# Four of eight feed-forward batches moved in slices into the second half of an attention loop

## What is computed

```python
def _L0_xattn_ref(hidden_states, key_value_states, ...):
    h_q = (rmsnorm(hidden_states) @ w_q.T).reshape(b, lq, H, DH)   # H = 32, DH = 128
    h_k = (key_value_states @ w_k.T).reshape(b, lk, H, DH)
    h_v = (key_value_states @ w_v.T).reshape(b, lk, H, DH)
    score = softmax(where(mask, h_q h_k^T + position_bias, -inf))
    return hidden_states + (score h_v) @ w_out.T

def _L0_ffn_ref(x, w_gate, w_up, w_down):          # HIDDEN 512, INTER 1376
    def fake_quant(t, axis):
        s = maximum(max(abs(t), axis) / 127, 1e-8)
        return clip(round(t / s), -128, 127) * s
    gate, up = qlinear(x, w_gate), qlinear(x, w_up)   # both operands fake_quant
    return qlinear(silu(gate) * up, w_down)

# third layer: per position, the 76 largest of 128 context channels (top_k) choose
# which rows of x are "crucial"; each part is reduced by max and mean over channels
```

## Time and profile before

| | |
|---|---|
| median of 3 runs | 1130.78 us (1128.15 to 1132.11) |
| the profiled execution | 1128.72 us |
| its span, first to last instruction | 1127.0 us |
| PE busy | 1005.8 us (89% of the span) |
| DVE busy | 697.8 us (62%) |
| ACT busy | 512.3 us (45%) |
| POOL busy | 496.3 us (44%) |
| mean granted clock of TensorE | 0.964 |

### The profile page before, as it was taken

How to read it: one execution, slowest core, us unless ns; L and a number is a source line. 1 busy time by engine, 2 the same in 40 slices (tenths; PEclk the granted TensorE clock), 3 DMA queues, 4 the chain that set the end, 5 groups by cost and what they waited for, 6 DMA issues and landing times. The chain is left out here.

```text
span 1127.0 us, 19424 instructions
## 1 busy us (share of the span) xinstructions
PE 1005.8 (89%) x6010; PEld 852.9 (76%) x6010; DVE 697.8 (62%) x1835; ACT 512.3 (45%) x1333; POOL 496.3 (44%) x370
## 2 busy tenths in 40 slices
PE   3798999999999999999999999999999976665455
PEld 2687888888888888888888888888888863332343
DVE  6676777777677677675444444444444479998375
ACT  2334344444434434444444444444444455767342
POOL 4544545454444455434444444444454412554200
PEclk8898999999999999999999999999999999999578
DMA  5222222222222223223222232223223100000001
GB/s 212 75 80 80 80 80 79 79 86 93 88 79 79 79 79 105 80 93 118 94 94 93 94 101 102 102 99 102 92 92 114 58 16 20 1 0 1 0 1 75
DMA packets 50325, 87.22 MB, mean 77 GB/s; under 512 B 6320, under 2 KB 15152, under 8 KB 50288
## 3 DMA queue, kind: packets, MB, share of 16 engines
q1 hardware_dynamic: 50288, 86.76, 23.3%
HBM read 84.64 MB, written 2.10 MB: 77 GB/s over the span
## 5 line engine op out<-in xcount | busy, mean ns | idle before, releaser
L632 ACT ACTIVATE prob<-score,neg_max 128x128 f32<-128x128 f32 x256 | 99.8, 391 | 140.6 <-DVE neg_max L899 140.5
L966 DVE TENSOR_TENSOR aT_lo<-pT,aT_hi 128x512 fp32r<-128x512 f32 x64 | 44.2, 691 | 179.2 <-ACT aT_hi L572 179.1
L1221 PE MATMUL pX<-wv_lo,cT_hi 128*128 128x256 f32 x512 | 151.4, 296 | 0.7 <-ACT v_sb L572 0.7
L464 POOL TENSOR_TENSOR wq_lo<-raw_q,wq_hi 128x512 fp32r<-128x512 f32 x64 | 92.2, 1441 | 130.7 <-ACT wq_hi L572 130.6
L1222 PE MATMUL pX<-wv_hi,cT_lo 128*128 128x256 f32 x512 | 145.9, 285 | 0.0
L1223 PE MATMUL pX<-wv_hi,cT_hi 128*128 128x256 f32 x512 | 145.9, 285 | 0.0
L472 POOL TENSOR_TENSOR b_mask<-b_raw,mask_add 128x512 f32<-128x512 f32 x64 | 74.7, 1168 | 151.2 <-DVE score L896 151.2
L464 POOL TENSOR_TENSOR wv_lo<-raw_v,wv_hi 128x1024 fp32r<-128x1024 f32 x32 | 76.9, 2402 | 109.0 <-ACT wv_hi L572 109.0
L572 ACT ACTIVATE v_sb<-pX 128x512 f32<-128x512 f32 x64 | 38.2, 597 | 175.7 <-PE pX L1223 175.7
L860 DVE COPY k_sb<-pX 128x512 f32<-128x512 f32 x64 | 44.1, 688 | 112.9 <-PE pX L1223 112.9
L1221 PE MATMUL pX<-xT_lo,wq_hi 128*128 128x512 f32 x256 | 107.3, 419 | 4.3 <-DVE xT_lo L848 4.3
(11 more groups left out here) (213 smaller groups left out, 2407.2 us busy)
## 6 DMA issues: line engine op xcount, KB each, us to landing
raw_q<-in_wq SPq DMA_DIRECT2D x64, 256.0 KB, 3.5
raw_k<-in_wk SPq DMA_DIRECT2D x64, 256.0 KB, 3.4
raw_v<-in_wv SPq DMA_DIRECT2D x32, 512.0 KB, 3.9
raw_o<-in_wo SPq DMA_DIRECT2D x64, 256.0 KB, 2.7
b_raw<-in_bias SPq DMA_DIRECT2D x64, 64.0 KB, 3.1
f_raw<-in_w_down SPq DMA_DIRECT2D x4, 688.0 KB, 6.5
g_raw<-in_w_gate SPq DMA_DIRECT2D x16, 172.0 KB
g_raw<-in_w_up SPq DMA_DIRECT2D x16, 172.0 KB
```

The costliest lines, as they stand in the source:

```text
L464: g.tensor_tensor(w_lo[c][:], w_raw[c][:], w_hi[c][:].bitcast(F32), ALU.subtract).then_inc(s_w_lo[c], 1)
L632: e = a.activation(prob[:, b, :], score[:, b, :], ACT.Exp, bias=neg_max[:, b:b + 1], accum_out=row_sum[:, b:b + 1])
L966: v.tensor_tensor(aT_lo[:], pT[:], aT_hi[:].bitcast(F32), ALU.subtract).then_inc(s_a_lo, 1)
L1221: mm(dst, lh, rl, start=start, stop=False, skip_group_check=lint)
```

## The change

In the words of its author: feed-forward of the first four batches put in slices between the projections of the second half of attention; gate and up rows quantised in the first half.

- **Rows.** The 32 blocks of w_gate and w_up go from steps 32 to 63 to steps 0 to 31 (rows_of_gate, ahead of the top-k round).
- **Top-k.** Four steps instead of two for two tiles, over both halves: one filling of pick (j = 0, where j = n mod 4), two rounds in steps j = 0 to 2, one in j = 3, each step's first one ahead of prob. It is filled from the split context (cT_hi, cT_lo) instead of cT_raw.
- **w_down.** Steps 32 to 35, with one buffer f_raw; block 0 is loaded in the first half, block i + 1 after the loads of step 33 + i and ScalarE's f_q of block i. Its transposes are in steps 33 to 36 (banks pT and pX1), the row of steps sd_row in step 37.
- **Feed-forward of batch t = 0 to 3** over steps 38 + 6t + r (turn(n, r)): r = -2 statistics, -1 y and its integers, 0 transposes of y into pT, 0 to 2 gate into pX1 behind the values, 1 to 3 up into pT behind the outputs, 3 silu, 4 product, maximum and integers, 5 transposes of h, 6 down projection into pX0 and xr, 7 and 8 normalisation to z, 9 its transposes, 10 split on GpSimd, 11 maxima and sums. The z part is done for batches 0 to 2; batch 3's z is left to the tail. Each piece that borrows a bank adds a wait for its reader (first_bank_free, key_bank_free).
- **Tail.** ffn_step for batches 4 to 7 only; residual now comes ahead of it; GpSimd computes z of batches 0 to 2 again into the array that lies over attention's. Steps 32 to 63 are written out, no longer a loop.

```diff
-        DOWN_STEPS = (H, H + 1, STEPS - 2, STEPS - 1)
+        FFN_FROM = H + 6
+        PERIOD = 6
+        DOWN_FROM = H
+        EARLY_Z = HB - 1
+        def turn(n, r):
+            t, rest = divmod(n - FFN_FROM - r, PERIOD)
+            return t if rest == 0 and 0 <= t < HB else None
...
@@ sync
+            for n in range(H, STEPS):
+                loads(n, n // 2, n % 2, n - H)
+                i = down_turn(n - 1)
+                if i is not None and i + 1 < KT:
+                    sp.wait_ge(s_f_q, i + 1)
+                    sp.dma_start(f_raw[:], w_down[(i + 1) * P:(i + 2) * P, :]).then_inc(s_f_in, 16)
...
@@ scalar
+                t = turn(n, 3)
+                if t is not None:
+                    act.wait_ge(s_e_gate, CHUNKS * (t + 1))
+                    a.activation(e_gate[:], e_gate[:], ACT.Silu).then_inc(s_e_silu, 1)
...
@@ vector
+            def early_bubble(n):
+                t = turn(n, -1)
+                if t is not None:
+                    dve.wait_ge(s_e_rstd, t + 1)
+                    v.tensor_scalar(y[:], xr[:, t, :], e_ymv[:, 0:1], e_yrs[:, 0:1], ALU.subtract, ALU.mult)
...
+                    v.tensor_scalar(y_mag[:], y[:], y_s[:, 2:3], MAGIC, ALU.mult, ALU.add).then_inc(s_e_y_mag, 1)
...
+                t = turn(n, 4)
+                if t is not None:
+                    dve.wait_ge(s_e_silu, t + 1)
+                    v.tensor_tensor(e_up[:], e_gate[:], e_up[:], ALU.mult)
+                    dve.drain()
+                    v.tensor_reduce(e_hs[:, 0:1], e_up[:], AX.X, ALU.max, apply_absolute_value=True)
...
+            def step(n, half, q, j, rows=False):
...
+                v.tensor_reduce(neg_max[:], score[:], AX.X, ALU.max, negate=True).then_inc(s_max_done, 1)
+                if rows:
+                    rows_of_gate(n)
+                early_bubble(n)
+                if j == 0:
+                    dve.drain()
+                    for r in range(2):
...
+                        v.scalar_tensor_tensor(out=pick[:, r, ::-1], in0=hi, scalar=-1.0, in1=lo,
+                                               op0=ALU.mult, op1=ALU.subtract)
+                pick_round(last=j == 3)
+                dve.wait_ge(s_exp_done, n + 1)
...
+                early_first_bank(n)
...
+                early_end(n)
+                dve.wait_ge(s_a_hi, n + 1)
+                v.tensor_tensor(aT_lo[:], pT[:], aT_hi[:].bitcast(F32), ALU.subtract).then_inc(s_a_lo, 1)
...
             v.memset(mv1[:], 0.0)
-            dve.drain()
+            residual(1)
             ffn_step(-2)
-            residual(1)
             ffn_step(-1)
...
@@ tensor
+            def early_query_bank(n):
+                t = turn(n, 6)
+                if t is not None:
+                    if unless_last(n + 1):
+                        pe.wait_ge(s_q, n + 2)
+                    pe.wait_ge(s_e_h_qT, 2 * t + 2)
+                    for k in range(IT):
...
+                        last = mm(pX0[:], e_hqT[0:deep, k * S:(k + 1) * S], wdT[0:deep, k, :],
+                                  start=k == 0, stop=k == IT - 1)
+                    last.then_inc(s_e_d_proj, 1)
```

More of the change, by code:

```diff
@@ L340, in live, with live_z @@
         def live(t):
-            return not isinstance(t, int) or 0 <= t < B
+            return 0 <= t < HB
+        def live_z(t):
+            return 0 <= t <= HB
         @block.sync
@@ L391, in _ @@
             load("o", 0, 0)
[L393 to L407, removed]
-                    if unless_last(n + 1):
-                        load("o", n + 1, head1)
-                    if odd and unless_last(n + 3):
-                        load("v", m + 2, (pair + 2) % (H // 2) if isinstance(pair, int) else pair + 2)
@@ new lines, in load_quad @@
+            def load_quad(q, rows):
+                for j in range(4):
+                    loads(4 * q + j, 2 * q + j // 2, j % 2, 4 * q + j, rows)
+            load_quad(0, 0)
+            with sp.Fori(1, 4) as q:
+                load_quad(q, 0)
+            sp.wait_ge(s_xT_lo, B)
+            sp.wait_ge(s_cT_lo, 2 * KT)
+            sp.wait_ge(s_mask_add, 1)
+            sp.dma_start(f_raw[:], w_down[0:P, :]).then_inc(s_f_in, 16)
+            with sp.Fori(4, 7) as q:
+                load_quad(q, 1)
@@ L680, in _ @@
-            for m in range(PAIRS - 2, PAIRS):
-                pair(m, m % 2, rows=True)
-            def down_tile(t):
-                cols = slice(t * P, (t + 1) * P)
-                first, second = (bank.rearrange("p (k s) -> p k s", s=P) for bank in wd_banks)
-                act.wait_ge(s_f_trans, 2 * t + 1)
-                copy(wdT[:, 0:8, cols], first).then_inc(s_f_out, 1)
-                act.wait_ge(s_f_trans, 2 * t + 2)
-                copy(wdT[:, 8:IT - 1, cols], second[:, 0:IT - 9, :])
-                copy(wdT[0:LAST, IT - 1, cols], second[0:LAST, IT - 9, :]).then_inc(s_f_out, 1)
@@ new lines, in quad @@
+            def quad(q, rows):
+                for j in range(4):
+                    step(4 * q + j, 2 * q + j // 2, j % 2, j // 2, rows)
+            quad(0, 0)
+            with act.Fori(1, 4) as q:
+                quad(q, 0)
+            act.wait_ge(s_xT_lo, B)
+            act.wait_ge(s_cT_lo, 2 * KT)
+            act.wait_ge(s_mask_add, 1)
+            with act.Fori(4, 7) as q:
+                quad(q, 1)
+            quad(7, 1)
+            for n in range(H, STEPS):
+                step(n, n // 2, n % 2, n // 2 % 2)
@@ L983, in maxima, with quad @@
+            def quad(q):
+                for j in range(4):
+                    step(4 * q + j, 0, q, j, rows=True)
+            dve.wait_ge(s_cT_lo, KT)
+            quad(0)
+            with dve.Fori(1, 7) as q:
+                quad(q)
+            quad(7)
+            dve.wait_ge(s_cT_lo, 2 * KT)
+            for n in range(H, STEPS):
+                step(n, 1, (n - H) // 4, n % 4)
             def maxima(t):
-                if live(t):
+                if live_z(t):
                     dve.wait_ge(s_sf, t + 1)
@@ new lines, in key_bank_free @@
+            def key_bank_free(n):
+                for j in range(CHUNKS):
+                    t = turn(n, j)
+                    if t is not None:
+                        pe.wait_ge(s_e_gate, CHUNKS * t + j + 1)
+                t = turn(n, 5)
+                if t is not None:
+                    pe.wait_ge(s_e_h_qT, 2 * t + 2)
+                t = turn(n, 9)
+                if t is not None and t < EARLY_Z:
+                    pe.wait_ge(s_e_zT, t + 1)
+                i = down_turn(n - 1)
+                if i is not None:
+                    pe.wait_ge(s_f_out, 2 * i + 2)
```

992 lines of the change are left out of this document (595 added, 397 removed).

## The result

The changed kernel takes 1190.78 us (median of 4 runs, 1187.02 to 1195.98) against 1130.24 us (4 runs, 1128.15 to 1132.11). The ratio is 1.054, 95% interval 1.049 to 1.059. The forecast was slower, at 1137 us with a range up to 1152. The direction was right; of the size, +60 us, one eighth was foreseen.

What follows compares the result with a forecast made beforehand. Attention was taken as bound by TensorE's own queue. TensorE work 36.3 us plus waits 25.6 less tail 54.1 gave +7.8 us, so 1137 us, with a range from 1114 to 1152.

Steps and rivals of the forecast that it cites:

- What bounds the kernel: Attention is bound by TensorE's own queue, so anything put into it costs its full length; the tail has TensorE room.
- First half, 3.3 us, range 0 to 5: Waits for prob in steps 0 to 31: eight j = 0 steps at 0.3 us, and 0.9 in step 2.
- The inequality: In an attention step, work between neg_max and prob is free until prob ends over 8.3 us after queries start.
- Rival 3: Slower by far: the clock falls if two close 2 us waits count as one; +16 us, 1153 us, chance 0.09.
- Steps 42 to 60, 7.8 us: Steps 42, 48, 54, 60: hidden product makes prob 1.5 us late, 2.4 with copies of pick; 7.8 us, from 4 to 10.
- Steps 49 and 55, 3.2 us: y, maxima and a round together make the chain about 10.3 against 8.7 us: 1.6 each, from 0 to 5 in all.
- w_down, 9.1 us: Steps 33 to 35: with one f_raw buffer VectorE waits for blocks, delaying aT_lo; 9.1 us, from 4 to 14.
- TensorE's length, 38.5 with the insertions: Feed-forward work put into attention: 36.3 us of TensorE, none hidden, plus 2.2 us for some 44 insertions.
- The second half as a whole: Steps 32 to 63: 36.3 and 2.2 us for TensorE, 20.1 for waits, less some 13 for departed rows; 45.6 in all.
- Tail, -54.1 us: After attention: four feed-forward steps go, 58.6 us; the start of the tail gets 4.5 us longer.
- The rule weighed: VectorE instructions with two SBUF inputs or in two-port mode wait for GpSimd's; without it, product waits 4 not 7.8 us.
- Slower: Whole kernel slower than before: chance 0.42 as summed and 0.09 with the clock; the slower case alone 1134.5 to 1150 us.

Runs made afterwards that it cites:

- experiment 9: Experiment 8's kernel with only the first of eleven down-projection matmuls made in steps 44, 50, 56 and 62: 1112.60 us.
- experiment 1: Changed kernel with the load of gate or up rows issued ahead of raw_q and raw_k: 1172.33 us, ratio 1.038 to the kernel before.
- experiment 2: Changed kernel with copies of pick and the first top-k round behind the copy to pT_sb, load still late: 1154.63 us, ratio 1.022 to the kernel before.
- experiment 6: Changed kernel with the first top-k round behind pT_sb only in steps 42, 48, 54 and 60: 1187.23 us, ratio 1.049 to the kernel before.
- experiment 7: Changed kernel with earlier row load, rounds behind pT_sb (first half, product steps), two w_down buffers, later z tiles: 1131.07 us, ratio 1.0005 to the kernel before.
- experiment 8: Experiment 7's kernel with maxima and first top-k round behind pT_sb in steps 49, 55 and 61 too: 1122.68 us, ratio 0.9925 to the kernel before.
- experiment 5: Changed kernel with two buffers for w_down blocks, 1 and 3 going into the tile e_gate: 1178.78 us, ratio 1.044 to the kernel before.
- experiment 4: Changed kernel with GpSimd's three z tiles behind the tail's first two reciprocal roots: 1186.83 us, ratio 1.051 to the kernel before.
- experiment 3: Changed kernel with the row load ahead of raw_q and raw_k and the rounds behind the copy to pT_sb: 1145.51 us, ratio 1.014 to the kernel before.

## Why the prediction was right or wrong

**What bounds the kernel** was right. TensorE's own queue bounds attention wherever `prob` is in time, and experiment 9 shows that its length is then paid in full. In the late steps of the changed kernel the chain ahead of `prob` bounds it.

**First half, 3.3 us, range 0 to 5: this step failed.** Beside some 13 us for the rows' own TensorE time, which leave the second half again, the first half cost 50 us more. The inequality was the right tool, and it was used wrongly in three ways.
- It took the rows to be in time. In the kernel before, the load of a block is issued as soon as the buffer is free, one step ahead in SyncE's list and 8 to 13 us ahead of `score` in the trace; in the changed kernel it stands in the list of the step that needs it, behind raw_k, and came 3.6 to 5.1 us ahead of `score` in the steps in which VectorE waited. The text of the change shows this, and I had costed the move of the block on VectorE and not that of its load on SyncE. Mended alone it was worth 18 us by the medians, 30 in the profiled execution (experiment 1).
- It put the j = 0 steps at 0.3 us late and went on as if that were the risk. A chain that ends 0.3 us from its deadline and beside three GpSimd instructions is not a cost of 0.3: any delay lets the next instruction fall on the next lock. Mended alone, by moving the rounds, it was worth 36 us by the medians, 45 of the first half (experiment 2). `prob` came 9.4 to 11.7 us behind `score` in these steps, where my 8.6 behind the queries is 7.4 behind `score`. By these rows the range should have reached to stalls of 3 us, with the slower work behind them.
- It priced waits and not the clock behind them, save in step 33. That was 16.6 us of the first half. Rival 3 had the clock and, for eight late steps, the price of 16 us, at a chance of 0.09; but it asked for two waits close together, where single stops were enough. The reading behind it, that the clock falls after 3.79 us and not after 2.34, was of two stops: in the same trace no slow matmul follows the stop of 3.17 in step 0 (value matmuls 0.12 us apart behind 57.59).

**Steps 42 to 60, 7.8 us:** measured 10.5 (2.67, 2.91, 1.17, 3.78). Right in kind, at the upper end in size. **Steps 49 and 55, 3.2 us:** measured 0 in the changed kernel. Experiments 6 and 7 show that the chain can be late there, by 3.5 and 3.3 us, twice my 1.6 each; experiment 8 takes these stalls away. In the changed kernel the stalls of steps 48 and 54 had hidden them: TensorE came to `prob` 1.4 us later, and `y_mag` was not held (rows in experiment 6). The two terms were not to be added.

**w_down, 9.1 us:** 7.5 went when the second buffer came back (experiment 5). It stood in steps 33 to 36, in one 1.31 for the residual beside it, and in three waits for aT_lo of 1.96, 0.92 and 2.09, not in one of 6.2.

**TensorE's length, 38.5 with the insertions:** experiment 8 shows it best, since its mean granted clock is 1.00 in both halves:

```profile
49.00:499.20 450.20, 443.01 (x2759) 391.49 (x2758) 281.86 (x801) 211.99 (x565) 220.14 (x153) 1.00 0.29 93
499.20:957.70 458.50, 448.33 (x2703) 380.14 (x2701) 295.55 (x744) 216.73 (x548) 201.45 (x149) 1.00 0.24 77
```

TensorE is busy for 443.0 + 448.3 = 891.3 us in attention, 849.5 before: +41.9, 3.4 above my term. Where the 3.4 lie is not shown. My 0.05 us for each insertion has no row behind it; in experiment 8 the weight loads that begin a slice in pT stood idle for 0.26 us each, 24 times, but an idle weight load is not time lost by the matmuls, and this was not tried.

**The second half as a whole** came out near its sum, 47.4 for 45.6, in part by luck: steps 42 to 60 and TensorE's length were above their terms (2.7 and 3.4), steps 49 and 55 and w_down below (3.2 and 1.6).

**Tail, -54.1 us:** -47.0. The last outputs did start 1.3 sooner, and four batches fewer gave 58.2 us from the first `down` to the last, where 58.6 was the sum. The start was +8.9 and not +6.1: the sum put the three z tiles on GpSimd at nothing, and the first root waited behind them in the same queue (2.76 us; 1.9 of the tail came back in experiment 4). From the gate matmuls to the first `down` it took 1.2 more, the slow gate matmuls (4.74 for 2.48) among it, and 2.5 came behind the last `down` (79.1 us to the end, 76.6 before), which I did not trace further. Together -1.3 + 8.9 + 1.2 - 58.2 + 2.5 = -46.9.

**The rule weighed** fits every held instruction above. In step 12 the held ones are 2.2 us longer than free (1.06, 0.90 and 0.26 for `f_diag`, `g_mag` and `row_inv`), so without it the stop of 3.21 would have been about 1.0, an estimate from these rows. No run took GpSimd's work away, so the lock is read from coinciding ends and not tried by itself. I had let it into the product steps and not into the load's consequences.

**Chances.** Slower had 0.51, and the direction came true; but the 60 us are mostly a mechanism that the sum did not have. With the load and the rounds mended (experiment 3) the kernel was still 1.4% slower, so the direction was not luck alone. The range was too narrow: its upper end took the forecast's own bounds, and these assumed that no load of rows was late.

## What to carry to other kernels

When a block of work moves, follow its load as well: where is it issued, behind what, and how far ahead of its use is it against the landing time in the trace. A small operation put ahead of a deadline costs nothing until it slides into the next lock on another engine, so keep such work behind the deadline where the engine waits anyway; here that was worth more than the earlier load, and the two with a second buffer, later z tiles and later maxima turned 5.4% slower into 0.75% faster. After mending one stall, look at the step behind it before adding gains: here a stall in one step hid that of the next.

## What the hardware showed that I had not expected

- A multiplication of 128 x 4 elements took 1.16 us instead of 0.16 while GpSimd's subtraction ran, and `f_diag`, with one tensor input of 86 x 86, took 1.30 instead of 0.24.
- A load of 172 KB issued sixth in a burst of 1.5 MB within 3.1 us landed after 6.8 us; two places further ahead (experiment 1) VectorE waited 2.7 us in 4 steps for the up rows, instead of 14.0 in 11, and no longer for the gate rows.
- Behind 13 of the 14 stops of 2.6 us and more that `prob` caused in the changed kernel came some 3.5 us at half speed (254.49 to 257.88 in step 12), so that the stop of 3.2 us cost about 1.6 more. But the length of the stop does not decide it. Steps 24 and 28 both stopped for 2.90 us and took 15.60 and 17.75; the stretches just behind these stops, with the granted clock near the end of the row:

```profile
440.90:443.60 2.70, 2.70 (x26) 2.70 (x25) 1.83 (x8) 0.00 (x0) 0.00 (x0) 1.00 0.57 181
500.50:503.20 2.70, 2.70 (x15) 2.70 (x15) 1.74 (x7) 0.00 (x0) 0.00 (x0) 0.50 0.30 99
```

  Experiment 8 had a slow stretch behind a stop of 1.99 us in step 0. The Trainium skill (TensorE: Matmul & The Clock Gate, Part 1) says that the lower clock is the default and that activity releases it. The slow matmuls behind the 13 stops agree; why that of step 24 was spared is not shown.
- The same first half, with its late load, took 496.6 to 503.7 us in four kernels. That a schedule near its locks is noisy for that reason fits the 0.05 us of step 49 and the 2 us between steps 24 and 28, but was not tried.
